# First feed-forward: ScalarE copies the first expert's rows, and the gate's last operation goes behind the masked outputs

## The chip, the cores and the metric

The kernel runs on one core of a Trainium2 chip. The metric is the device time of one launch in microseconds (us). Three runs of the kernel before gave 2103.96, 2107.25 and 2112.59 us, median 2107.25 us. Five engines work side by side, each through its own list of instructions in order: TensorE (PE, with its weight loads PEld), VectorE (DVE), ScalarE (ACT), GpSimd (POOL) and SyncE (SP, which issues transfers here). They meet only at semaphores: a producer counts one up, a consumer waits until it has reached a value.

## What is computed

A stack of four layers, each with an attention and a gated feed-forward, over 64 sequences of 64 tokens with 128 features. Each layer adds `tanh(gate) * block(layernorm(x))` to `x`. The change touches only the first feed-forward, an attention whose values and outputs go through one of 8 experts for each token and head:

```python
q = (x @ w_q).reshape(b, n, HEADS, DIM_HEAD).transpose(0, 2, 1, 3)      # 8 heads of 64
k = (x @ w_k).reshape(b, n, HEADS, DIM_HEAD).transpose(0, 2, 1, 3)
gates = jax.nn.sigmoid((x @ w_gate).reshape(b, n, HEADS, EXPERTS).transpose(0, 2, 1, 3))
sel = jnp.argmax(gates, axis=-1)
gm = jax.nn.one_hot(sel, EXPERTS, dtype=x.dtype) * gates
values = jnp.einsum('bhne,ehdk,bnd->bhnk', gm, value_experts, x)
sim = jnp.einsum('bhid,bhjd->bhij', q * SCALE, k)
sim = jnp.where(causal_mask, jnp.finfo(sim.dtype).min, sim)
attn = jax.nn.softmax(sim, axis=-1)
out = jnp.einsum('bhij,bhjk->bhik', attn, values)
out = jnp.einsum('bhne,ehkd,bhnk->bhnd', gm, output_experts, out)
return out.sum(axis=1)
```

## The kernel before

The 4096 tokens are 32 tiles of 128 (two sequences each), and 4 tiles make a group: 8 groups, of which groups 1 to 6 run as one loop. `l0_ffn` writes the list of each engine by hand, and these lists set the order. Count for tile t of group g:

- **Values.** TensorE multiplies the tile by the value weights of each of the 8 experts (`expert_values`, L1011, two passes of one multiplication each), into three PSUM banks in turn. VectorE takes them out in `pick`: a plain copy of expert 0 into `val` (L1228), then seven predicated copies (L1233), each of which overwrites the heads that chose this expert. Each pick waits for the one before it, since all write the same rows; TensorE may write expert e only when the bank's last content is taken.
- **Scores.** `scores` (L1021, L1027), then on VectorE `softmax`: row maximum (L1242) and difference (L1245); on ScalarE `exp` (L1141); on VectorE `totals` (L1251 to L1256, sum, reciprocal, times the gate) and `scale_probs` (L1262), placed behind the first and the second predicated copy of the next tile. TensorE turns the probabilities (L1037), ScalarE copies them (`copy_pT`, L1148), TensorE multiplies by the gated values (`values`, L1053), ScalarE copies the result (`copy_oT`, L1154). GpSimd multiplies the picked values by the gate (L955).
- **Once a group.** In tile 0, ScalarE also copies the turned one-hots (`copy_onehots`, L1161), from which SyncE makes the masks by transfers; in tile 1, VectorE applies a norm (L247) and ScalarE copies its turned rows (L271).
- **End of a group.** TensorE computes the next group's logits and projects its q and k (L1002), which ScalarE copies. VectorE's `pick_experts` makes the one-hots from the logits and ends with the gate's last operation (L1218): gate = 0.5 * tanh + 0.5. That one waits for the tanh (L1134), which ScalarE computes behind its last k copy. Only then come the 32 masked outputs (`masked_outputs`, L1271, z = oT * mask, in three buffers), each of which TensorE multiplies by an output expert's weights into one accumulator (`output_experts`, L1062). ScalarE copies the accumulator (L1183), and the next group's tile 0 follows on TensorE and VectorE.

Of the kernel before, what the change touches and what calls it, by code (L numbers as in the profile page):

```python
# [78 lines left out]
def count(n):  # L79

    return n + 1
# [767 lines left out]
def l0_ffn(core, nc, d):  # L849
# [17 lines left out]
    with ExitStack() as ctx:  # L867
# [36 lines left out]
                                                                sem("oh_turned"), sem("ohT_ready"))  # L904
        qk_done, qk_copied = sem("qk_done"), sem("qk_copied")
        ve_done, pick_done, v2_ready = sem("ve_done"), sem("pick_done"), sem("v2_ready")
        score_done, sub_done, exp_done, tot_done = sem("score_done"), sem("sub_done"), sem("exp_done"), sem("tot_done")
        p_turned, pT_ready, pv_done, prob_ready = sem("p_turned"), sem("pT_ready"), sem("pv_done"), sem("prob_ready")
        oT_ready, z_done = sem("oT_ready"), sem("z_done")
# [6 lines left out]
        with nc.Block() as block:  # L916
# [19 lines left out]
            @block.gpsimd  # L936
            def _(pool):
                nc.gpsimd.tensor_copy(causal[:, :], core.const("caus_n")).then_inc(setup_done, 1)
                nc.gpsimd.memset(oh_bf[:, :, :], 0.0).then_inc(setup_done, 1)

                def stage(u):
                    after(pool, ve_done, u * G * E)
                    nc.gpsimd.tensor_copy(xs[:, :], core.xnT[:, bass.ds(u * GT, GT)]).then_inc(xs_ready, 1)

                gate = top[:, 2, :].rearrange("p (t h) -> p t h", t=G)

                def gate_values(g, t):
                    n = g * G + t
                    pool.wait_ge(pick_done, count((n + 1) * E))
                    after(pool, pv_done, n - 1)  # L950
                    for b in range(2):
                        for a in range(2):
                            r = slice(b * SEQ, (b + 1) * SEQ)
                            after(pool, v2_ready, n * 4 + 2 * b + a)
                            nc.gpsimd.tensor_tensor(  # L955
                                v2[a * SEQ:(a + 1) * SEQ, t % 2, b, :, :],
                                val[r, t % 2, :, :].rearrange("p (c a) k -> p c a k", a=2)[:, :, a, :],
                                bcast(gate[r, t, :].rearrange("p (c a) -> p c a", a=2)[:, :, a], 2, HD),
                                ALU.mult).then_inc(v2_ready, 1)
                    pool.wait_ge(v2_ready, count(n * 4 + 4))  # L960

                def group(g, more):
                    for t in range(1, G):
                        if t == G - 1 and more:
                            stage(g + 1)
                        gate_values(g, t)
                    if more:
                        gate_values(g + 1, 0)
                        norm_gpsimd(core, nc, pool, ns, g)

                stage(0)
                norm_gpsimd(core, nc, pool, edge, 0)
                gate_values(0, 0)
                group(0, True)
                pool.wait_ge(edge.ready, count(1))
                with pool.Fori(1, GROUPS - 1) as g:
                    group(g, True)
                group(GROUPS - 1, False)

            @block.tensor  # L980
            def _(pe):
# [12 lines left out]
                def project(u, chunks):  # L994

                    for i in chunks:
                        c = i % C
                        if i < 2:
                            after(pe, pick_done, u * G * E)
                        else:  # L1000
                            pe.wait_ge(qk_copied, count(u * 2 * C + i - 1))
                        nc.tensor.matmul(work[i % 2][:, :], (wq, wk)[i // C][:, c * P:(c + 1) * P],  # L1002
# [2 lines left out]
                def expert_values(g, t, between=None, later=None):  # L1005
                    for e in range(E):
                        n = (g * G + t) * E + e
                        if e == 2 and t == 0:
                            pe.wait_ge(y_ready, count(g))
                        after(pe, pick_done, n - 1 if e < 2 else n - 2)  # L1010
                        nc.tensor.matmul(value_banks[e % 3][:, :], xs[:, t * P:(t + 1) * P], ve[:, e, :],  # L1011
                                         start=True, stop=True).then_inc(ve_done, 1)
                        if e == 2 and between:
# [42 lines left out]

                def output_experts(g):
                    pe.wait_ge(y_ready, count(g))
                    pe.wait_ge(pick_done, count((g + 1) * G * E))
                    for n in range(C * E):  # L1060
                        pe.wait_ge(z_done, count(g * C * E + n + 1))
                        nc.tensor.matmul(acc[:, :], oe[:, n % E, n // E, :], z[:, n % Z, :], start=(n == 0),  # L1062
# [54 lines left out]
            def _(act):  # L1117
# [8 lines left out]
                def copy_k(u, chunks):  # L1126
                    after(act, score_done, u * G)
                    for c in chunks:
                        act.wait_ge(qk_done, count(u * 2 * C + C + c + 1))
                        nc.scalar.activation(kT[:, c, :], work[c % 2][:, :], ACT.Copy).then_inc(qk_copied, 1)  # L1130

                def gate_tanh(u):
                    act.wait_ge(top_ready, count(u + 1))
                    nc.scalar.activation(top[:, 1, :], top[:, 0, :], ACT.Tanh, scale=0.5).then_inc(tanh_done, 1)  # L1134
# [27 lines left out]

                def group(g, more, normed=True):
                    for t in range(G - 1):
                        copy_pT(g, t)
                        exp(g, t + 1)
                        copy_oT(g, t)
# [14 lines left out]
                    act.wait_ge(y_turned, count(g))  # L1182
                    nc.scalar.activation(yT[:, :], acc[:, :], ACT.Copy).then_inc(y_ready, 1)  # L1183
                    if more:
                        exp(g + 1, 0)

                copy_q(0, range(C))
                copy_k(0, range(C))
                gate_tanh(0)
                edge_scalar(core, nc, act, edge, misc)  # L1190
                exp(0, 0)
                group(0, True, False)
                with act.Fori(1, GROUPS - 1) as g:
                    group(g, True)
# [3 lines left out]
            def _(dve):  # L1198
# [4 lines left out]
                def pick_experts(u):  # L1203
# [9 lines left out]
                    after(dve, oh_turned, u)  # L1213
                    nc.vector.tensor_copy(oh_bf[:, :, 0:H * E], oh[:, :, :].rearrange("p (t h) e -> p t (h e)", t=G))\
                        .then_inc(oh_ready, 1)
                    dve.wait_ge(tanh_done, count(u + 1))

                    ch.link(nc.vector.tensor_scalar(top[:, 2, :], top[:, 1, :], 0.5, 0.5, ALU.mult, ALU.add))  # L1218
                    ch.done()

                def pick(g, t, between=()):
                    for e in range(E):
                        n = (g * G + t) * E + e
                        dve.wait_ge(ve_done, count(n + 1))
                        w3 = value_banks[e % 3][:, :].rearrange("p (h k) -> p h k", h=H)
                        if e == 0:
                            after(dve, v2_ready, (g * G + t - 1) * 4)
                            nc.vector.tensor_copy(val[:, t % 2, :, :], w3).then_inc(pick_done, 1)  # L1228
                        else:
                            dve.wait_ge(pick_done, count(n))  # L1230
                            dve.sem_inc(may_pick, 1)
                            m_e = bcast(oh[:, t * H:(t + 1) * H, e], 2, HD).bitcast(I32)
                            nc.vector.copy_predicated(val[:, t % 2, :, :], m_e, w3).then_inc(pick_done, 1)  # L1233
                        if 0 < e <= len(between):
                            between[e - 1]()

                def softmax(g, t):
# [47 lines left out]
                def group(g, more, normed=True):  # L1285
# [5 lines left out]
                    totals(g, G - 1)  # L1291
                    scale_probs(g, G - 1)
                    if more:
                        pick_experts(g + 1)
                    masked_outputs(g)
                    if more:
                        pick(g + 1, 0)
                    add_to_x(g, more)
                    if more:
                        softmax(g + 1, 0)  # L1300

                edge_measure(core, nc, dve, edge)
                pick_experts(0)
                edge_apply(core, nc, dve, edge)
                pick(0, 0)
                softmax(0, 0)
# [2106 lines left out]
```

## Time and profile before

| what | value |
|---|---|
| three runs, median | 2107.25 us |
| the profiled execution, its own time | 2104.33 us |
| its span, first to last instruction | 2102.2 us |
| mean granted TensorE clock | 0.950 |
| busy share of the span: PE, DVE, ACT, POOL | 91%, 73%, 40%, 34% |

The span is the profiled execution without its start and end (2.1 us). "Busy" is time in which an engine had an instruction in it. "Granted clock" is the TensorE clock that the chip gave: 1.00 is 2.4 GHz, 0.5 is 1.2 GHz. A row of the timeline has the start in us, the duration, the engine, the line, the operation with output and inputs, how many were merged, and in brackets how long the engine had been idle before it and who ended that.

### The profile page before, as it was taken

The numbers are of one execution on the slowest core, as the hardware profiler recorded it, in microseconds if no ns is written. First come the engines' busy times: TensorE is split into PE (matmuls) and PEld (weight loads), VectorE is DVE, ScalarE is ACT, GpSimd is POOL, SyncE is SP. The second block draws the span as 40 slices with busy tenths as digits, with TensorE's granted clock in tenths as the row PEclk, the third lists the DMA queues.
The fourth block names the chain that finished last, engine by engine and source line by source line (L and its number), as shares of the span: only waits on it lengthen the run. The fifth ranks groups of instructions, "written<-read, shape, count | busy, mean of one in ns | idle before, by whom it ended". The sixth has DMA issues, their size and how long they took to land. (4 is left out here: it accounts for less than half of the span.)

```text
span 2102.2 us, 41789 instructions
## 1 busy us (share of the span) xinstructions
PE 1916.6 (91%) x14339; PEld 1025.3 (49%) x14339; DVE 1537.1 (73%) x3177; ACT 836.1 (40%) x1500; POOL 721.2 (34%) x953
## 2 busy tenths in 40 slices
PE   5869999998998988999999999979998999989975
PEld 3734444444444444555555554435663444436641
DVE  4767877877877776777777776857785666768978
ACT  6622112112012005666666663315652223225655
POOL 2541111102112105677676774455730000013222
PEclk9569999999999999999999999989998999999985
DMA  5403203212132041000000000000002524221001
GB/s 140 149 1 82 63 21 79 45 39 61 35 66 61 20 113 76 2 2 1 0 0 0 0 2 1 1 8 15 15 7 80 129 73 118 63 64 20 16 1 40
DMA packets 60080, 89.74 MB, mean 43 GB/s; under 512 B 23720, under 2 KB 42024, under 8 KB 55472
## 3 DMA queue, kind: packets, MB, share of 16 engines
q1 hardware_dynamic: 59952, 88.10, 17.1%
q8 instruction: 72, 1.18, 0.2%
q14 instruction: 56, 0.46, 0.1%
HBM read 80.91 MB, written 2.97 MB: 40 GB/s over the span
## 5 line engine op out<-in xcount | busy, mean ns | idle before, releaser
L955 POOL TENSOR_TENSOR l0f_v<-l0f_val,l0f_top 64x256 f32<-64x256 f32 x128 | 78.2, 611 | 484.2 <-DVE l0f_val L1233 476.7
L1062 PE MATMUL l0f_acc<-l0f_z,w_all 128*128 128x512 f32 x512 | 228.5, 608 | 15.0 <-DVE l0f_z L1271 15.0
L1011 PE MATMUL l0f_work<-w_all,l0f_xs 128*128 128x512 f32 x384 | 183.4, 600 | 15.0 <-DVE l0f_val L1228 14.2
L1062 PEld LDWEIGHTS l0f_acc<-l0f_z,w_all 128*128 128x128 f32 x512 | 99.0, 195 | 143.9 <-issue 123.1
L255 POOL TENSOR_SCALAR var_eps<-mean_var 128x4 f32<-128x4 f32 (+1 forms) x64 | 16.8, 263 | 375.8 <-DVE mean_var L239 373.6
L1477 PE MATMUL l1x_proj_v<-l1x_wvo,l1x_cs 128*64 128x512 f32 x512 | 139.2, 622 | 0.0
L1233 DVE COPY_PREDICATED l0f_val<-l0f_oh,l0f_work 128x512 f32<-128x512 int32 x160 | 116.7, 729 | 22.8 <-PE l0f_work L1011 7.9
L2881 ACT ACTIVATE l2f_act_g<-l2f_pg 128x512 f32<-128x512 f32 x104 | 61.6, 594 | 146.3 <-PE l2f_pu L2816 134.3
L2824 PE MATMUL l2f_acc<-l2f_hid,w_all 128*128 128x512 f32 x208 | 107.4, 598 | 10.2 <-DVE l2f_hid L2962 10.2
L2956 DVE TENSOR_TENSOR l2f_hu<-l2f_act_g,l2f_pu 128x512 f32<-128x512 f32 x104 | 71.1, 684 | 60.3 <-ACT l2f_act_g L2881 58.8
L1011 PEld LDWEIGHTS l0f_work<-w_all,l0f_xs 128*128 128x128 f32 x384 | 66.1, 190 | 87.8 <-issue 32.2
L2815 PE MATMUL l2f_pg<-xnT_all,w_all 128*128 128x512 f32 x208 | 108.7, 605 | 0.0
L2535 ACT ACTIVATE a_probT<-a_pT 128x512 f32<-128x512 f32 x128 | 76.3, 596 | 81.1 <-PE a_pT L2412 81.1
L1271 DVE TENSOR_TENSOR l0f_z<-l0f_oT,l0f_first_mask 128x512 f32<-128x512 f32 x128 | 87.2, 691 | 28.4 <-PE l0f_acc L1062 22.6
L2816 PE MATMUL l2f_pu<-xnT_all,w_all 128*128 128x512 f32 x208 | 107.9, 601 | 0.0
L1402 POOL TENSOR_TENSOR l1x_rs_q<-l1x_ms_q,minus_half 128x8 f32<-128x8 f32 x64 | 104.7, 1636 | 5.7 <-POOL l1x_ms_q L1398 0.8
L1411 POOL TENSOR_TENSOR l1x_rs_k<-l1x_ms_k,minus_half 128x8 f32<-128x8 f32 x64 | 104.7, 1636 | 5.3
L1271 DVE TENSOR_TENSOR l0f_z<-l0f_oT,w_all 128x512 f32<-128x512 f32 x128 | 88.6, 692 | 21.2 <-PE l0f_acc L1062 20.9
L1631 ACT ACTIVATE l1x_vo<-l1x_proj_v 128x512 f32<-128x512 f32 x128 | 76.4, 597 | 62.5 <-PE l1x_proj_v L1477 62.5
L1712 DVE TENSOR_TENSOR l1x_nm_q<-l1x_proj_q,l1x_rs_q 128x512 f32<-128x512 f32 x64 | 44.3, 692 | 77.8 <-POOL l1x_rs_q L1402 77.8
L1415 POOL TENSOR_TENSOR l1x_prob<-l1x_prob,l1x_inv 128x512 f32<-128x512 f32 x64 | 66.7, 1042 | 98.2 <-DVE l1x_inv L1741 98.2
L1183 ACT ACTIVATE xn<-l0f_acc 128x512 f32<-128x512 f32 x8 | 4.8, 597 | 237.9 <-PE l0f_acc L1062 237.9
(400 smaller groups left out, 4375.2 us busy)
## 6 DMA issues: line engine op xcount, KB each, us to landing
l0f_first_mask<-onehots SPq DMA_DIRECT2D x32, 512.0 KB, 5.8
w_all<-onehots SPq DMA_DIRECT2D x32, 512.0 KB, 11.8
w_all<-combination SPq DMA_DIRECT2D x40, 256.0 KB, 5.1
w_all<-in_weights SPq DMA_DIRECT2D x1, 4640.0 KB, 16.8
l0x_m_b<-running_max SPq DMA_DIRECT2D x16, 256.0 KB, 4.3
w_all<-combination SPq DMA_DIRECT2D x16, 224.0 KB, 4.3
w_all<-combination SPq DMA_DIRECT2D x16, 192.0 KB, 4.1
w_all<-combination SPq DMA_DIRECT2D x16, 160.0 KB, 4.1
```

The lines of the kernel that those rows point to most:

```text
L955: nc.gpsimd.tensor_tensor(v2[a * SEQ:(a + 1) * SEQ, t % 2, b, :, :], val[r, t % 2, :, :].rearrange("p (c a) k -> p c a k", a=2)[:, :, a, : ...
L1011: nc.tensor.matmul(value_banks[e % 3][:, :], xs[:, t * P:(t + 1) * P], ve[:, e, :], start=True, stop=True).then_inc(ve_done, 1)
L1062: nc.tensor.matmul(acc[:, :], oe[:, n % E, n // E, :], z[:, n % Z, :], start=(n == 0), stop=(n == C * E - 1)).then_inc(acc_done, 1)
L1233: nc.vector.copy_predicated(val[:, t % 2, :, :], m_e, w3).then_inc(pick_done, 1)
L1271: nc.vector.tensor_tensor(z[:, n % Z, :], oT[:, n // E, :], masks[n // E][:, n % E, :], ALU.mult)\
L1402: nc.gpsimd.tensor_tensor(rs_q[:, :], ms_q[:, 1, :], core.half[:, 0:HU], ALU.pow).then_inc(rs_q_done, 1)
L1411: nc.gpsimd.tensor_tensor(rs_k[:, :], ms_k[:, 1, :], core.half[:, 0:HU], ALU.pow).then_inc(rs_k_done, 1)
L1477: ins = nc.tensor.matmul(proj_v[a * SEQ:(a + 1) * SEQ, :], cs[:, j // 4, at:at + SEQ], wvo[:, h, a, :], start=True, stop=True)
L1631: nc.scalar.activation(vo[:, j % 2, b, :, :], proj_v[:, :].rearrange("p (c d) -> p c d", c=C), ACT.Copy)\
L2815: nc.tensor.matmul(pg[n % 3][:, :], wg[:, c * P:(c + 1) * P], x_of(g), start=True, stop=True)
L2816: nc.tensor.matmul(pu[n % 3][:, :], wu[:, c * P:(c + 1) * P], x_of(g), start=True, stop=True)\
L2824: nc.tensor.matmul(acc[:, :], wd[:, c * P:(c + 1) * P], hid[:, n % 3, :], start=(c == 0), stop=(c == CH - 1)).then_inc(acc_done, 1)
```

## The change

Three things are moved.

1. The copy of expert 0 into `val` leaves VectorE's `pick` and becomes `copy_first` on ScalarE, with a semaphore of its own, `first_copied`. The picks now count 7 a tile. TensorE's fourth expert of a tile waits for `first_copied`, and so does VectorE's first predicated copy.
2. `copy_first` of the next tile stands at the head of what ScalarE does for a tile: ahead of `copy_pT` and of the next tile's exponential. In tile 0 the group's first exponential, which stood at the end of the group before, comes behind the copy for tile 1. The copy for tile 0 of the next group is behind the accumulator's copy.
3. The gate's last operation is cut out of `pick_experts` (`gate_halves`) and stands behind the 32 masked outputs, ahead of the next group's picks.

```diff
                 def expert_values(g, t, between=None, later=None):
                     for e in range(E):
                         n = (g * G + t) * E + e
+                        if e == 0 and t == 0:
+                            pe.wait_ge(qk_copied, count((g + 1) * 2 * C))
                         if e == 2 and t == 0:
                             pe.wait_ge(y_ready, count(g))
-                        after(pe, pick_done, n - 1 if e < 2 else n - 2)
+                        if e == 3:
+                            pe.wait_ge(first_copied, count(g * G + t + 1))
+                        else:
+                            after(pe, pick_done, (g * G + t) * PICKS + (-1, 0, -2, 0, 1, 2, 3, 4)[e])
...
+                def copy_first(g, t):
+                    n = g * G + t
+                    act.wait_ge(ve_done, count(n * E + 1))
+                    after(act, v2_ready, (n - 1) * 4)
+                    nc.scalar.activation(val[:, t % 2, :, :], value_banks[0][:, :].rearrange("p (h k) -> p h k", h=H),
+                                         ACT.Copy).then_inc(first_copied, 1)
...
                 def group(g, more, normed=True):
                     for t in range(G - 1):
+                        copy_first(g, t + 1)
+                        if t == 0:
+                            exp(g, 0)
                         copy_pT(g, t)
                         exp(g, t + 1)
                         copy_oT(g, t)
...
                     if more:
-                        exp(g + 1, 0)
+                        copy_first(g + 1, 0)
...
+                def gate_halves(u, ch):
                     dve.wait_ge(tanh_done, count(u + 1))
-
                     ch.link(nc.vector.tensor_scalar(top[:, 2, :], top[:, 1, :], 0.5, 0.5, ALU.mult, ALU.add))
                     ch.done()
...
                     if more:
-                        pick_experts(g + 1)
+                        ch = pick_experts(g + 1)
                     masked_outputs(g)
                     if more:
+                        gate_halves(g + 1, ch)
                         pick(g + 1, 0)
                     add_to_x(g, more)
```

How the lists of the engines change is shown at three places. First VectorE at the end of group 0, from the one-hots' cast to the next group's picks. Before (lines L1218 gate, L1271 masked outputs, L1228 first expert's copy):

```order
L1214 CAST l0f_oh_bf<-l0f_oh 128x4x64 [waits counter1_24,counter1_20]
L1218 TENSOR_SCALAR l0f_top<-l0f_top 128x32 [waits counter1_22]
L1271 TENSOR_TENSOR l0f_z<-l0f_oT,l0f_first_mask 128x512 [waits mask_loaded0,counter1_42,counter1_39,counter1_20]
L1271 TENSOR_TENSOR l0f_z<-l0f_oT,l0f_first_mask 128x512 [waits counter1_42] x7
...
L1271 TENSOR_TENSOR l0f_z<-l0f_oT,l0f_first_mask 128x512 [waits counter1_42] x7
L1228 COPY l0f_val<-l0f_work 128x512 [waits counter1_30,counter1_28]
L1233 COPY_PREDICATED l0f_val<-l0f_oh,l0f_work 128x512 [waits counter1_28,counter1_29]
```

And now, at the same place (L1237 gate, L1289 masked outputs, L1251 predicated copy; counter1_40 is `oT_ready`, counter1_22 `tanh_done`, counter1_31 `first_copied`):

```order
L1231 CAST l0f_oh_bf<-l0f_oh 128x4x64 [waits counter1_24,counter1_20]
L1289 TENSOR_TENSOR l0f_z<-l0f_oT,l0f_first_mask 128x512 [waits counter1_43,mask_loaded0,counter1_40]
L1289 TENSOR_TENSOR l0f_z<-l0f_oT,l0f_first_mask 128x512 [waits counter1_43] x7
...
L1289 TENSOR_TENSOR l0f_z<-l0f_oT,l0f_first_mask 128x512 [waits counter1_43] x7
L1237 TENSOR_SCALAR l0f_top<-l0f_top 128x32 [waits counter1_22]
L1251 COPY_PREDICATED l0f_val<-l0f_oh,l0f_work 128x512 [waits counter1_31,counter1_20,counter1_28]
```

The gate's operation and its wait for ScalarE moved from ahead of 32 instructions to behind them, and the copy of expert 0 is gone from the list.

Second, VectorE at a tile's turn, from the difference of one tile to the totals, before:

```order
L1245 TENSOR_TENSOR l0f_diff<-l0f_score,l0f_mx 128x2x4x64 [waits counter1_48]
L1228 COPY l0f_val<-l0f_work 128x512 [waits counter1_28]
L1233 COPY_PREDICATED l0f_val<-l0f_oh,l0f_work 128x512 [waits counter1_28,counter1_29]
L1251 TENSOR_REDUCE l0f_tot<-l0f_prob 128x8 [waits counter1_33]
L1253 RECIPROCAL l0f_tot<-l0f_tot 128x8 [waits counter1_49]
```

and now (counter1_34 is `exp_done`):

```order
L1263 TENSOR_TENSOR l0f_diff<-l0f_score,l0f_mx 128x2x4x64 [waits counter1_34,counter1_49]
L1251 COPY_PREDICATED l0f_val<-l0f_oh,l0f_work 128x512 [waits counter1_28,counter1_31]
L1269 TENSOR_REDUCE l0f_tot<-l0f_prob 128x8 [waits counter1_34]
L1271 RECIPROCAL l0f_tot<-l0f_tot 128x8 [waits counter1_50]
```

One instruction instead of two stands between the difference and the sum of its exponentials, and the first predicated copy waits for ScalarE.

Third, ScalarE in the loop body, tiles 0 and 1, before (L1148 turned probabilities, L1141 exponential, L1154 output, L1161 one-hots, L271 norm):

```order
L1148 ACTIVATE l0f_probT<-l0f_turn 128x512 [waits counter1_37]
...
L1141 ACTIVATE l0f_prob<-l0f_diff 128x512 [waits counter1_34,counter1_35,counter1_32]
...
L1154 ACTIVATE l0f_oT<-l0f_po 128x4x128 [waits counter1_40]
...
L1161 ACTIVATE l0f_ohT<-l0f_misc 128x512 [waits onehots_stored]
L1148 ACTIVATE l0f_probT<-l0f_turn 128x512 [waits counter1_37,counter1_35]
...
L1154 ACTIVATE l0f_oT<-l0f_po 128x4x128 [waits counter1_40,counter1_37]
...
L271 ACTIVATE xnT_all<-l0f_misc 128x512
```

and now (L1143 `copy_first`, L1162 turned probabilities, L1155 exponential, L1168 output, L1175 one-hots):

```order
L1143 ACTIVATE l0f_val<-l0f_work 128x512 [waits counter1_30]
...
L1155 ACTIVATE l0f_prob<-l0f_diff 128x512 [waits counter1_35,counter1_36,counter1_33]
L1162 ACTIVATE l0f_probT<-l0f_turn 128x512 [waits counter1_38,counter1_36]
...
L1155 ACTIVATE l0f_prob<-l0f_diff 128x512 [waits counter1_35,counter1_36,counter1_33]
...
L1168 ACTIVATE l0f_oT<-l0f_po 128x4x128 [waits counter1_41]
...
L1175 ACTIVATE l0f_ohT<-l0f_misc 128x512 [waits onehots_stored]
...
L1143 ACTIVATE l0f_val<-l0f_work 128x512 [waits counter1_30]
L1162 ACTIVATE l0f_probT<-l0f_turn 128x512 [waits counter1_38,counter1_36]
...
L271 ACTIVATE xnT_all<-l0f_misc 128x512
...
L1143 ACTIVATE l0f_val<-l0f_work 128x512 [waits counter1_30]
```

The copy for tile 1 comes ahead of tile 0's exponential; the copy for tile 2 is behind the exponential of tile 1, the output copy and the one-hots; the copy for tile 3 is behind the exponential of tile 2, the output copy and the norm's rows.

## Rows read from the trace of the kernel before

**Rows 1.** Stretches of one group each: us, busy time by engine, clock, DMA share, GB/s.
```profile
221.30:302.20 80.90, 75.46 (x445) 36.43 (x444) 63.14 (x110) 13.29 (x24) 11.65 (x19) 1.00 0.25 54
302.20:385.30 83.10, 77.29 (x445) 37.00 (x445) 63.38 (x110) 13.35 (x25) 11.65 (x19) 0.98 0.24 52
...
630.10:712.90 82.80, 77.26 (x446) 37.02 (x445) 63.23 (x110) 13.34 (x25) 11.65 (x19) 0.98 0.24 51
```

**Rows 2.** Who waited for whom, stretch 140 to 780: us, times, longest.
```profile
PE l0f_acc L1062 <- DVE l0f_z L1271: 15.0, 8, 1.9
```

**Rows 3.** Timeline where group 3's masked outputs begin: start, duration, engine, line.
```profile
515.69 1.98 PE L1002 MATMUL l0f_work<-xnT_all,w_all 128*128 x4
519.61 4.11 PE L1062 MATMUL l0f_acc<-l0f_z,w_all 128*128 128x512 f32 x5 [1.94 <-DVE l0f_z L1271]
...
515.81 0.60 ACT L1154 ACTIVATE l0f_oT<-l0f_po 128x512 f32<-128x512 f32 x1 [0.49 <-PE l0f_po L1053]
...
518.46 0.18 DVE L1218 TENSOR_SCALAR l0f_top<-l0f_top 128x32 f32<-128x32 f32 x1 [3.84 <-ACT l0f_top L1134]
518.87 1.89 DVE L1271 TENSOR_TENSOR l0f_z<-l0f_oT,l0f_first_mask 128x512 f32<-128x512 f32 x3 [0.22 <-DVE l0f_top L1218]
```

**Rows 4.** Timeline, last group, where no gate operation stands ahead.
```profile
760.84 0.60 ACT L1154 ACTIVATE l0f_oT<-l0f_po 128x512 f32<-128x512 f32 x1 [2.15 <-PE l0f_po L1053]
...
761.47 1.89 DVE L1271 TENSOR_TENSOR l0f_z<-l0f_oT,l0f_first_mask 128x512 f32<-128x512 f32 x3 [4.12 <-ACT l0f_oT L1154]
```

**Rows 5.** Line L1062 in two groups: us, PE busy, clock, DMA share, GB/s.
```profile
438.50:466.20 27.70, 27.66 (x64) 1.00 0.18 38
519.60:549.00 29.40, 29.39 (x64) 0.94 0.16 36
```

**Rows 6.** Timeline, VectorE and TensorE, tiles 0 and 1 of that group.
```profile
467.29 0.69 DVE L1228 COPY l0f_val<-l0f_work 128x512 f32<-128x512 f32 x1 [2.86 <-PE l0f_work L1011]
...
477.41 0.69 DVE L1245 TENSOR_TENSOR l0f_diff<-l0f_score,l0f_mx 128x512 f32<-128x512 f32 x1
478.02 0.69 DVE L1228 COPY l0f_val<-l0f_work 128x512 f32<-128x512 f32 x1
478.85 0.73 DVE L1233 COPY_PREDICATED l0f_val<-l0f_oh,l0f_work 128x512 f32<-128x512 int32 x1
479.47 0.67 DVE L1251 TENSOR_REDUCE l0f_tot<-l0f_prob 128x8 f32<-128x512 f32 x1
...
478.77 1.98 PE L1011 MATMUL l0f_work<-w_all,l0f_xs 128*128 128x512 f32 x4 [1.53 <-DVE l0f_val L1228]
```

**Rows 7.** Timeline, VectorE, tile 3, whose totals have no pick ahead.
```profile
508.02 0.69 DVE L1245 TENSOR_TENSOR l0f_diff<-l0f_score,l0f_mx 128x512 f32<-128x512 f32 x1
509.41 0.69 DVE L1251 TENSOR_REDUCE l0f_tot<-l0f_prob 128x8 f32<-128x512 f32 x1 [0.69 <-ACT l0f_prob L1141]
```

**Rows 8.** Timeline, ScalarE and VectorE, tiles 2 and 3 of that group.
```profile
487.90 0.58 ACT L1154 ACTIVATE l0f_oT<-l0f_po 128x512 f32<-128x512 f32 x1
488.38 0.59 ACT L1161 ACTIVATE l0f_ohT<-l0f_misc 128x512 bf16<-128x512 bf16 x1
...
490.05 0.73 DVE L1233 COPY_PREDICATED l0f_val<-l0f_oh,l0f_work 128x512 f32<-128x512 int32 x1
...
499.60 0.59 ACT L271 ACTIVATE xnT_all<-l0f_misc 128x512 f32 x1
...
500.21 0.73 DVE L1233 COPY_PREDICATED l0f_val<-l0f_oh,l0f_work 128x512 f32<-128x512 int32 x1 [0.22 <-PE l0f_work L1011]
```

**Rows 9.** Timeline, ScalarE and VectorE, tiles 2 and 3 of group 0.
```profile
164.27 0.59 ACT L1161 ACTIVATE l0f_ohT<-l0f_misc 128x512 bf16<-128x512 bf16 x1
...
164.66 0.73 DVE L1233 COPY_PREDICATED l0f_val<-l0f_oh,l0f_work 128x512 f32<-128x512 int32 x1 [0.31 <-PE l0f_work L1011]
...
173.62 0.58 ACT L1154 ACTIVATE l0f_oT<-l0f_po 128x512 f32<-128x512 f32 x1
...
174.30 0.73 DVE L1233 COPY_PREDICATED l0f_val<-l0f_oh,l0f_work 128x512 f32<-128x512 int32 x1 [0.31 <-PE l0f_work L1011]
```

More of the change, by code:

```diff
@@ L906, in l0_ffn @@
         ve_done, pick_done, v2_ready = sem("ve_done"), sem("pick_done"), sem("v2_ready")
+        first_copied = sem("first_copied")
+        PICKS = E - 1
         score_done, sub_done, exp_done, tot_done = sem("score_done"), sem("sub_done"), sem("exp_done"), sem("tot_done")
@@ L948, in gate_values @@
                     n = g * G + t
-                    pool.wait_ge(pick_done, count((n + 1) * E))
+                    pool.wait_ge(pick_done, count((n + 1) * PICKS))
                     after(pool, pv_done, n - 1)
@@ L998, in project @@
                         if i < 2:
-                            after(pe, pick_done, u * G * E)
+                            after(pe, pick_done, u * G * PICKS)
                         else:
@@ L1058, in output_experts @@
                     pe.wait_ge(y_ready, count(g))
-                    pe.wait_ge(pick_done, count((g + 1) * G * E))
+                    pe.wait_ge(pick_done, count((g + 1) * G * PICKS))
                     for n in range(C * E):
@@ L1189, in _ @@
                 gate_tanh(0)
+                copy_first(0, 0)
                 edge_scalar(core, nc, act, edge, misc)
-                exp(0, 0)
                 group(0, True, False)
@@ L1215, in pick_experts @@
                         .then_inc(oh_ready, 1)
+                    return ch
+                def gate_halves(u, ch):
                     dve.wait_ge(tanh_done, count(u + 1))
@@ L1221, in pick @@
                 def pick(g, t, between=()):
-                    for e in range(E):
-                        n = (g * G + t) * E + e
-                        dve.wait_ge(ve_done, count(n + 1))
+                    n = g * G + t
+                    for e in range(1, E):
+                        dve.wait_ge(ve_done, count(n * E + e + 1))
                         w3 = value_banks[e % 3][:, :].rearrange("p (h k) -> p h k", h=H)
-                        if e == 0:
-                            after(dve, v2_ready, (g * G + t - 1) * 4)
-                            nc.vector.tensor_copy(val[:, t % 2, :, :], w3).then_inc(pick_done, 1)
-                        else:
[L1230 to L1234, printed above, removed]
+                        if e == 1:
+                            dve.wait_ge(first_copied, count(n + 1))
+                        else:
+                            dve.wait_ge(pick_done, count(n * PICKS + e - 1))
+                        dve.sem_inc(may_pick, 1)
+                        m_e = bcast(oh[:, t * H:(t + 1) * H, e], 2, HD).bitcast(I32)
+                        nc.vector.copy_predicated(val[:, t % 2, :, :], m_e, w3).then_inc(pick_done, 1)
+                        if e <= len(between):
                             between[e - 1]()
@@ L1302, in _ @@
                 edge_measure(core, nc, dve, edge)
-                pick_experts(0)
+                gate_halves(0, pick_experts(0))
                 edge_apply(core, nc, dve, edge)
```

## The prediction

> **What bounds the kernel now.** I read the chip's clock by stretches first: it splits the first feed-forward into its 8 groups. A steady group takes 80.9 us with TensorE busy for 75.5, VectorE for 63.1 and ScalarE for only 13.3 [rows 1]. So TensorE is the bound, ScalarE has room, and a microsecond is won only where TensorE waits. The stretches also show two kinds of group: 80.9 us at clock 1.00, and 82.8 to 83.1 us at 0.98 [rows 1].
>
> The list of waits was next: TensorE waits for the first masked output 8 times, 15.0 us in all, at most 1.94 [rows 2]. Seven times 1.94 are 13.6; the rest is the last group's, which has no next group behind it. The timeline shows why [rows 3]. The output copy ends at 515.81 + 0.60 = 516.41, and VectorE has everything that a masked output needs. It sits idle for 3.84 us all the same, because the gate's operation at 518.46 stands ahead and waits for ScalarE's tanh, which is queued behind the last k copies. The first masked output begins at 518.87. TensorE is through with its projections at 517.67 and stands for 1.94.
>
> In three groups (those of 302, 466 and 630) this wait costs twice: behind it TensorE gets the lower of its clocks for a while. The 64 passes of L1062 take 29.4 us at a mean clock of 0.94 in the group of 466, and 27.7 at 1.00 in the one before [rows 5]: 1.7 us.
>
> In tiles 1 to 3 VectorE sets the pace, with TensorE waiting for it for up to 1.53 us [rows 6]. There the copy of expert 0 costs VectorE 478.85 - 478.02 = 0.83 us per tile, since the first predicated copy waits for it to end [rows 6].
>
> **The change part by part.**
>
> *Gate behind the masked outputs.* What the masked outputs wait for last is then the output copy. The last group, which has no gate operation there, shows the lag: copy ends at 760.84 + 0.60 = 761.44, first masked output at 761.47 [rows 4]; the masks had landed there too. So in a steady group the first one starts at 516.45 instead of 518.87 and ends at 517.14, ahead of TensorE's 517.67. The wait of 1.94 is gone, in 7 groups: **-13.6**. The gate's 0.18 us now stand behind the last masked output, where VectorE was idle for 2.86 us before the copy at 467.29 [rows 6], and the tanh is long done: 0. GpSimd needs the gate only behind the picks. If the cover were gone it would cost 7 x 0.2 = 1.4.
>
> *The clock.* The group of 466 lacks about 0.06 x 29.4 = 1.8 us of clock in L1062's stretch [rows 5], and a group at 0.98 lacks 0.02 x 83 = 1.7 in all [rows 1]: the low stretch stands behind the wait and nowhere else. With the wait gone I take them as gone: 3 x 1.7, **-5.1**. Bounds: 0, if something else brings the clock down, to -5.1.
>
> *Copy for tile 0 on ScalarE.* VectorE waited for TensorE there anyway (2.86 us [rows 6]), and both go on at one expert per 0.86 us: 0. ScalarE copies behind the accumulator's copy, well before expert 1 is there.
>
> *Copy for tile 1, ahead of the exponential.* TensorE's expert 0 is ready while VectorE still adds to x, so the first predicated copy starts where the plain copy did, 478.02. The totals, then, can't begin before the exponential is done. Where no pick stands between, difference to totals takes 509.41 - 508.02 = 1.39 [rows 7]; before it was 479.47 - 477.41 = 2.06 here [rows 6]. Gain 0.67, not 0.83.
>
> *Copy for tile 2.* It stands behind the exponential, the output copy and the one-hots. ScalarE starts such operations one per 0.5 us (487.90 to 488.38 [rows 8]). The copy starts at 488.38 + 0.50 - 0.67 = 488.21, ends 0.60 later at 488.81, and with 0.15 for the semaphore the first predicated copy starts at 488.96 instead of 490.05: 1.09 ahead.
>
> *Copy for tile 3.* It stands behind the exponential, the output copy and the norm's copy: 499.60 + 0.50 - 1.09 + 0.60 + 0.15 = 499.76 instead of 500.21. Only 0.45 is left of the lead, because VectorE waits for ScalarE here where it waited for TensorE before. TensorE's fourth and later experts follow the picks with the same lead. So 0.45 a group, groups 1 to 7 (the last is built alike): **-3.1**.
>
> *Group 0* has no norm on VectorE behind which the copies could hide. Tile 2: 164.27 + 0.50 + 0.60 + 0.15 = 165.52 against 164.66, 0.86 late. Tile 3: 173.62 + 0.86 + 0.50 + 0.60 + 0.15 = 175.73 against 174.30, 1.43 late [rows 9]. **+1.4**.
>
> The step from one ScalarE operation to the next is the unsure figure. Taken at its full 0.60 plus 0.10, each of the three steps from the exponential to the copy is 0.2 longer and the end 0.1: 0.7 later in all. Tile 2 is then 1.09 - 0.7 = 0.4 ahead, tile 3 499.60 + 0.50 - 0.4 + 0.60 + 0.15 + 0.7 = 501.15, 0.94 late, 6.6 in 7 groups; group 0 has 0.7 more in tile 2 and some 0.5 in tile 3, 2.7. That makes the tiles +9.3 instead of -1.7. On the other side, if the copies never come late, tiles 1 to 3 gain about 0.67 + 0.83 and what TensorE leaves of the third, 1.5 a group in 7 groups and 0 in group 0: -10.5. I take the middle, since the rows of two neighbouring operations show the 0.5 directly.
>
> ScalarE's copy of 128x512 from PSUM takes 0.60 (the output copy at 515.81 [rows 3]) against 0.69 on VectorE [rows 6]. The Trainium skill advises the opposite ("ScalarE: Activation LUTs", rules for kernel authors): plain element-wise work belongs on VectorE, which it calls up to about three times as fast in bf16. This operand is fp32, and the rows show ScalarE the quicker one here. At three times 0.69, 2.07 us, the copies of tiles 2 and 3 would each be 1.47 later in 8 groups, +23.5, and the whole +3 instead of a gain; the trace disagrees with that.
>
> **Sum:** -13.6 - 5.1 - 3.1 + 1.4 = -20.4. The profiled execution took 2104.33 us (span 2102.2 and 2.1 around it), so 2083.9; it lies 2.9 below the median of the three runs, 2107.25. From the median, 2107.25 - 20.4 = **2087**.
>
> **The rivals.**
>
> *The tiles gain in full* (ScalarE never late): -13.6 - 5.1 - 10.5 = -29.2, 2078. For: ScalarE is idle most of the time. Against: its three operations ahead of the copy all start at the same moment, when the difference is done.
>
> *The low clock stays or comes elsewhere*: -15.3, 2092. For: it came in only three of the seven groups with the same wait, so something besides the wait decides.
>
> *ScalarE's queue at its long step*: -18.7 + 9.3 = -9.4, 2098. For: each operation waits for its own semaphores. Against: the 0.48 between neighbours [rows 8].
>
> *The change doesn't open the wait*: masked outputs wait for something else at 516 (a mask, the accumulator), and only the tiles' -1.7 is left, 2105.5. Against: rows 4.
>
> *Slower*: the waits move into the tiles and pull the clock down there. TensorE's fourth expert no longer waits, but the fifth waits some 0.8 us for the first pick, the sixth 0.9 for the second, in 21 tiles (three in each of 7 groups), and longer with the long step. Each low stretch costs 1.7. Starting from the -9.4 of the long step, 6 such stretches eat the gain, and 12 make it slower by over 0.5%. Two in each of 7 groups: -9.4 + 23.8 = +14.4, 2121.7. For: three stretches behind a wait of 1.94. Against: the wait of 1.53 in tile 1 [rows 6] left the clock at 1.00 in the groups of 80.9.
>
> **How the numbers follow.** Forecast as worked out, 2083 to 2092: 0.50. Tiles in full, 0.12. Low clock stays, 0.15. Long step, 0.13. Nothing opened, 0.04. Slower, 0.06. What a measurement of this kernel can tell from no change is about 0.5%, 10.5 us, so faster means below 2096.7: 0.50 + 0.12 + 0.15 and a fourth of the long step's, 0.80. Same: the rest of the long step and the unopened wait, 0.14. Slower by over 10.5: 0.06. The range 2079 to 2099 takes in the forecast, the low clock, most of the long step and about half of the full gain, and leaves out under 2 in 10.
>
> **What will show it.** Right: no wait of L1062's first pass for VectorE in groups 0 to 6; the first masked output within 0.1 us of the output copy's end; clock 1.00 in the groups of 302, 466 and 630; all steady groups at 78.5 us (80.9 - 1.94 - 0.45); difference to totals 1.4 us in tile 1; the first predicated copies of tiles 2 and 3 waiting for `copy_first`; group 0 longer in its tiles by about 1.4. Wrong: TensorE still waiting at 516 to 518 for a masked output; a clock below 1.00 inside the tiles; steps of 0.7 or more between the exponential, the output copy and `copy_first`; or a later stage that gives back what this one wins, though each begins only when the one before it is through.

## The result and the profile after

| | before | changed |
|---|---|---|
| median | 2111.98 us (7 runs) | 2097.23 us (7 runs) |
| lowest to highest | 2103.96 to 2118.68 | 2092.68 to 2100.41 |
| span of the profiled execution | 2102.2 | 2093.9 |

The ratio is 0.9934, 95% interval 0.9919 to 0.9949, so 0.7% faster: the medians differ by 14.8 us, and the interval is 10.8 to 17.1 us. Forecast were 20.4 us less, 2087 us, range 2079 to 2099.

The wait that the change was about is gone. TensorE, VectorE and ScalarE in the timeline of the changed kernel where group 4's masked outputs begin [answers to rows 3, which are group 4's too; their heading counts it as group 3]; a row has start, duration, engine, line, operation, and in brackets the idle time before it and who ended it:

```profile
509.77 1.98 PE L1004 MATMUL l0f_work<-xnT_all,w_all 128*128 x4
511.59 27.63 PE L1069 MATMUL l0f_acc<-l0f_z,w_all 128*128 128x512 f32 x64
...
508.48 0.29 DVE L1231 CAST l0f_oh_bf<-l0f_oh 128x256 bf16<-128x256 f32 x1
510.70 2.64 DVE L1289 TENSOR_TENSOR l0f_z<-l0f_oT,l0f_first_mask 128x512 f32<-128x512 f32 x4 [1.93 <-ACT l0f_oT L1168]
...
536.68 0.69 DVE L1289 TENSOR_TENSOR l0f_z<-l0f_oT,l0f_first_mask 128x512 f32<-128x512 f32 x1 [0.17 <-PE l0f_acc L1069]
537.29 0.17 DVE L1237 TENSOR_SCALAR l0f_top<-l0f_top 128x32 f32<-128x32 f32 x1
541.18 0.73 DVE L1251 COPY_PREDICATED l0f_val<-l0f_oh,l0f_work 128x512 f32<-128x512 int32 x1 [3.71 <-PE l0f_work L1018]
...
509.88 0.60 ACT L1168 ACTIVATE l0f_oT<-l0f_po 128x512 f32<-128x512 f32 x1 [0.49 <-PE l0f_po L1060]
```

VectorE begins at 510.70, 0.22 behind the output copy's end (510.48; the prediction had asked for 0.1), and TensorE goes from its projections to the 64 passes with no wait. Between 140 and 780 us it now waits once for a masked output, 1.5 us in the last group, where it had waited 8 times and 15.0 us. The gate's 0.17 us stand in an idle stretch of 3.7 us.

By stretches, three groups of the changed kernel (us, then busy time of PE, PEld, DVE, ACT, POOL, the clock, DMA share, GB/s) [answers to rows 1]:

```profile
222.71:301.24 78.53, 75.42 (x445) 36.32 (x444) 60.51 (x106) 15.44 (x29) 11.68 (x19) 1.00 0.25 56
459.10:539.26 80.16, 76.87 (x445) 37.14 (x444) 60.48 (x106) 15.44 (x29) 11.67 (x19) 0.98 0.25 53
539.26:618.11 78.85, 75.45 (x445) 36.33 (x444) 60.51 (x106) 15.46 (x28) 11.68 (x19) 1.00 0.25 54
```

A steady group takes 78.8 us instead of 80.9 to 81.1 (forecast 78.5), and one group has a low stretch instead of three. But look at VectorE and ScalarE: VectorE has 2.6 us less to do and ScalarE 2.1 more, and of that nothing shows in the 78.8: the wait alone accounts for what a steady group gained.

The same group of 459 by its two parts, from the accumulator's copy to the first output product and from there to the next copy (us, PE busy, clock, DMA share, GB/s), and then the first part of the group behind it [answers to rows 5]:

```profile
459.10:511.60 52.50, 49.21 (x381) 0.97 0.29 61
511.60:539.30 27.70, 27.70 (x66) 1.00 0.17 38
539.30:590.40 51.10, 47.70 (x380) 1.00 0.30 63
```

The low stretch has moved: not behind the masked outputs' start any more, but inside the first part, in the tiles, where it costs 1.4 us (52.5 against 51.1). VectorE and ScalarE in tiles 1 to 3 of the group of 539 [answers to rows 6 and 8]:

```profile
550.52 0.69 DVE L1263 TENSOR_TENSOR l0f_diff<-l0f_score,l0f_mx 128x512 f32<-128x512 f32 x1
551.24 0.72 DVE L1251 COPY_PREDICATED l0f_val<-l0f_oh,l0f_work 128x512 f32<-128x512 int32 x1
551.91 0.69 DVE L1269 TENSOR_REDUCE l0f_tot<-l0f_prob 128x8 f32<-128x512 f32 x1
...
562.19 0.72 DVE L1251 COPY_PREDICATED l0f_val<-l0f_oh,l0f_work 128x512 f32<-128x512 int32 x1 [0.29 <-ACT l0f_val L1143]
...
570.12 0.69 DVE L1263 TENSOR_TENSOR l0f_diff<-l0f_score,l0f_mx 128x512 f32<-128x512 f32 x1
573.08 0.73 DVE L1251 COPY_PREDICATED l0f_val<-l0f_oh,l0f_work 128x512 f32<-128x512 int32 x1 [2.27 <-ACT l0f_val L1143]
...
570.84 0.63 ACT L1155 ACTIVATE l0f_prob<-l0f_diff 128x512 f32<-128x512 f32 x1 [3.79 <-DVE l0f_diff L1263]
571.38 0.58 ACT L1168 ACTIVATE l0f_oT<-l0f_po 128x512 f32<-128x512 f32 x1
571.86 0.59 ACT L271 ACTIVATE xnT_all<-l0f_misc 128x512 f32 x1
572.34 0.60 ACT L1143 ACTIVATE l0f_val<-l0f_work 128x512 f32<-128x512 f32 x1
```

Difference to totals is 1.39 us in tile 1, as forecast. In tile 3 VectorE waits 2.27 us for the copy, which has three of ScalarE's operations ahead of it, each 0.48 to 0.54 behind the one before. Where VectorE had waited for TensorE in the kernel before, it now waits for ScalarE.

TensorE's second wait in tile 1 of the kernel before (the first, 1.53 us, is in rows 6), and both waits of the changed kernel:

```profile
481.43 1.12 PE L1011 MATMUL l0f_acc<-w_all,l0f_xs 128*128 128x512 f32 x2 [0.68 <-DVE l0f_val L1233]
```

```profile
552.02 1.12 PE L1018 MATMUL l0f_work<-w_all,l0f_xs 128*128 128x512 f32 x2 [0.99 <-DVE l0f_val L1251]
...
553.96 1.12 PE L1018 MATMUL l0f_acc<-w_all,l0f_xs 128*128 128x512 f32 x2 [0.82 <-DVE l0f_val L1251]
```

### The profile page after: what moved, and what is told of

It reads as the page before. It is cut to its first block and busy times, and to the rows that moved or that the text cites. A ratio compares the mean times of both kernels' runs of the same rounds, so it can differ in the third digit from the quotient of the medians.

```text
span 2093.9 us, 41926 instructions
## 1 busy us (share of the span) xinstructions
PE 1922.9 (92%) x14337; PEld 1031.1 (49%) x14339; DVE 1514.5 (72%) x3145; ACT 853.1 (41%) x1532; POOL 722.6 (35%) x953
## 5 line engine op out<-in xcount | busy, mean ns | idle before, releaser
L1069 PE MATMUL l0f_acc<-l0f_z,w_all 128*128 128x512 f32 x512 | 223.1, 597 | 1.5 <-DVE l0f_z L1289 1.5
L1251 DVE COPY_PREDICATED l0f_val<-l0f_oh,l0f_work 128x512 f32<-128x512 int32 x160 | 116.6, 729 | 69.3 <-PE l0f_work L1018 33.3
L255 POOL TENSOR_SCALAR var_eps<-mean_var 128x4 f32<-128x4 f32 (+1 forms) x64 | 16.9, 264 | 381.7 <-DVE mean_var L239 379.5
L1289 DVE TENSOR_TENSOR l0f_z<-l0f_oT,l0f_first_mask 128x512 f32<-128x512 f32 x128 | 87.1, 691 | 36.7 <-PE l0f_acc L1069 18.1
L1289 DVE TENSOR_TENSOR l0f_z<-l0f_oT,w_all 128x512 f32<-128x512 f32 x128 | 88.6, 692 | 21.3 <-PE l0f_acc L1069 20.9
L2643 DVE TENSOR_REDUCE a_mx<-a_score 128x16 f32<-128x1024 f32 x64 | 77.6, 1212 | 23.8 <-PE a_score L2417 22.0
```

The lines of the kernel that those rows point to most:

```text
L1289: nc.vector.tensor_tensor(z[:, n % Z, :], oT[:, n // E, :], masks[n // E][:, n % E, :], ALU.mult)\
L2643: nc.vector.tensor_reduce(mx[:, t % 2, :], score[t % 2][:, :].rearrange("p (h k) -> p h k", h=H), AX.X, ALU.max).then_inc(max_done, 1)
```

## Experiments

Five theories were open: (a) the gain is the gate's alone; (b) the copies bring their part; (c) the low stretches hang on the wait; (d) the copies lose by their place in ScalarE's list; (e) the rest is lost in later stages. "First part" is from the accumulator's copy to the first output product, "second part" from there to the next copy.

**The gate's operation alone.** On the kernel before:

```diff
+                        if e == 0 and t == 0:
+                            pe.wait_ge(qk_copied, count((g + 1) * 2 * C))
...
-                        pick_experts(g + 1)
+                        ch = pick_experts(g + 1)
                     masked_outputs(g)
                     if more:
+                        gate_halves(g + 1, ch)
                         pick(g + 1, 0)
```

> The kernel before with only the gate's last operation behind the masked outputs (and the wait of the first expert's multiplication for ScalarE's last k copies, which that order needs); the copies of expert 0 stay on VectorE. My theory: TensorE's wait of 1.94 us at the first masked output goes in 7 groups and the low stretches of the clock behind it go too, so the steady groups' first part (accumulator copy to first output product) falls from 53.3 to 51.3 us, the first feed-forward from 647.5 us (first tanh to last accumulator copy) to about 629, and the time by 18.6 us, ratio 0.991. Rival, the later stages give back part of whatever this stage wins, by whatever reason: same stage time, but a ratio of 0.994 to 0.996 and the stretch behind the stage longer than 1310.6 us by 5 or more.

Measured: 2090.92 us against 2109.26, ratio 0.9912, interval 0.9894 to 0.9929. First and second part of a steady group at full clock, and ahead of them group 0's first part from its tanh on:

```profile
145.40:192.80 47.40, 46.82 (x376) 1.00 0.31 69
457.30:508.40 51.10, 47.57 (x380) 1.00 0.29 63
508.40:536.10 27.70, 27.70 (x66) 1.00 0.16 38
```

No group has a low stretch but the last. The first feed-forward took 628.0 us instead of 647.5, and the ratio is the 0.991 that was expected, not the 0.994 to 0.996 of the rival; the stretch behind this stage took 1315.5 us, though, which the last experiment takes up. So by the trace this edit alone brings 2.4 us more than the whole change (630.4; the intervals of the two ratios overlap). Of the 2.4, the changed kernel loses 1.7 in group 0 and 1.4 by its low stretch in a tile, and wins 0.6 in group 1. The steady first part, 51.1, is the same as the changed kernel's: in groups 3 to 6 the moved copies bring nothing.

**The copies alone.** The changed kernel with

```diff
-                        ch = pick_experts(g + 1)
+                        gate_halves(g + 1, pick_experts(g + 1))
                     masked_outputs(g)
                     if more:
-                        gate_halves(g + 1, ch)
                         pick(g + 1, 0)
```

> The changed kernel with the gate's last operation back ahead of the masked outputs, so that only the copies of expert 0 are moved. My theory: the wait of 1.94 us at the first masked output is back in 7 groups, the tiles of a steady group are shorter by only 0.2 us (53.3 to 53.1 in the first part), group 0's first part is 1.6 longer than before (49.3 to 50.9), and low stretches of the clock stay at about three; the time is the same as before within 0.2%. Rival, the copies are where the gain of the change comes from: 0.996 or less. Rival, the copies cost the missing part: 1.002 or more.

Measured: 2114.08 against 2109.26, ratio 1.0020, interval 1.0008 to 1.0032: slower, at the edge between my "same within 0.2%" and the rival's cost, and the rival is nearer. Group 0's first part is 51.1 us. Of the steady groups, one row of a first and one of a second part:

```profile
389.40:442.60 53.20, 47.97 (x381) 1.00 0.28 60
...
606.20:635.70 29.50, 29.50 (x65) 0.94 0.16 36
```

The first part is 53.2, as good as unchanged (53.3 before). The stage took 653.8 us instead of 647.5. The cost is group 0's 1.8 and more low stretches: five second parts have one instead of three, and one first part too, besides the last group's. I had expected about three. Why there are more is not shown.

**TensorE kept busy through the wait.** On the kernel before:

```diff
                         project(g + 1, range(C + 2, 2 * C))
+                        for _ in range(2):
+                            nc.tensor.matmul(turn[:, :], wq[:, 0:P], core.xnT[:, 0:GT], start=True, stop=True)
```

> The kernel before, with two extra multiplications of 128x512 (0.43 us a pass, two passes each) into a free bank behind the last k projection, whose result nobody reads: TensorE is busy for 1.7 of the 1.94 us that it waited for the first masked output. The masked outputs still begin behind the gate's operation. My theory: the first output product starts where it did (53.3 us behind the accumulator's copy), but the clock doesn't fall, so the second part of all groups is 27.7 us instead of 29.4 in three of them: 5 us less, ratio 0.9976. Rival, the low stretches have nothing to do with the wait: three groups with 29.4 us stay, ratio 1.000.

Measured: 2105.18 against 2109.26, ratio 0.9985, interval 0.9974 to 0.9995. TensorE and VectorE in the timeline, and the two parts of that group:

```profile
516.57 1.88 PE L1097 MATMUL l0f_turn<-xnT_all,w_all 128*128 128x512 f32 x4
518.67 2.84 PE L1062 MATMUL l0f_acc<-l0f_z,w_all 128*128 128x512 f32 x6 [0.22 <-DVE l0f_z L1273]
...
517.52 0.18 DVE L1220 TENSOR_SCALAR l0f_top<-l0f_top 128x32 f32<-128x32 f32 x1 [3.81 <-ACT l0f_top L1136]
```

```profile
465.40:518.70 53.30, 49.48 (x385) 1.00 0.28 60
518.70:546.40 27.70, 27.70 (x65) 1.00 0.18 38
```

The first product starts where it did, since VectorE still waits for the tanh, yet no second part but the last group's is 29.4 or longer: all are at clock 1.00. That is theory (c), shown by itself, in the seven groups of one profiled execution, and the interval of the ratio lies below 1. The stage is 643.3 us instead of 647.5, 4.2 less of 5 expected; the last group, whose low stretch is longer, takes back 1.0.

**The copies right behind the exponential.** On the changed kernel:

```diff
                     for t in range(G - 1):
-                        copy_first(g, t + 1)
                         if t == 0:
+                            copy_first(g, 1)
                             exp(g, 0)
                         copy_pT(g, t)
                         exp(g, t + 1)
+                        if t + 2 < G:
+                            copy_first(g, t + 2)
                         copy_oT(g, t)
```

> The changed kernel with the copies of expert 0 for tiles 2 and 3 moved ahead of the output copy: right behind the exponential of the tile before, so two of ScalarE's operations no longer stand before them. My theory: VectorE's wait for the copy goes from 0.3 us to 0 in tile 2 and from 2.3 to about 1.4 in tile 3, a steady group's first part falls from 51.2 to about 50.0 us, group 0's from 49.1 to about 47.5, and the time is some 10 us below the changed kernel, ratio to the kernel before 0.989. Rival, the output copy and what hangs on it (the turned probabilities, the next group's projections) are late then and take it back: first part 51.2 or more.

Measured: 2086.03 against 2109.26, ratio 0.9895, interval 0.9877 to 0.9914. Tile 3 on VectorE and ScalarE, and a steady group's two parts:

```profile
562.58 0.69 DVE L1265 TENSOR_TENSOR l0f_diff<-l0f_score,l0f_mx 128x512 f32<-128x512 f32 x1
564.93 0.73 DVE L1253 COPY_PREDICATED l0f_val<-l0f_oh,l0f_work 128x512 f32<-128x512 int32 x1 [1.66 <-PE l0f_work L1018]
...
563.31 0.63 ACT L1155 ACTIVATE l0f_prob<-l0f_diff 128x512 f32<-128x512 f32 x1 [3.80 <-DVE l0f_diff L1265]
563.95 0.60 ACT L1143 ACTIVATE l0f_val<-l0f_work 128x512 f32<-128x512 f32 x1
564.45 0.59 ACT L1168 ACTIVATE l0f_oT<-l0f_po 128x512 f32<-128x512 f32 x1
```

```profile
454.30:504.40 50.10, 47.23 (x380) 1.00 0.30 64
504.40:532.10 27.70, 27.70 (x66) 1.00 0.17 38
```

The copy is done at 564.55, and what VectorE waits for in tile 3 is TensorE again. The first part is 50.1 to 50.2 (50.0 expected) and group 0's 47.8 (from 49.1). Theory (d) holds, and the output copy that was pushed back costs little: at most the 0.1 to 0.2 us by which the first part missed what was expected.

**Picks counted by 8 again.** On that kernel; the thresholds of TensorE and GpSimd follow:

```diff
-                    n = g * G + t
                     for e in range(1, E):
-                        dve.wait_ge(ve_done, count(n * E + e + 1))
+                        n = (g * G + t) * E + e
+                        dve.wait_ge(ve_done, count(n + 1))
...
-                            dve.wait_ge(pick_done, count(n * PICKS + e - 1))
+                            dve.wait_ge(pick_done, count(n))
...
-                        nc.vector.copy_predicated(val[:, t % 2, :, :], m_e, w3).then_inc(pick_done, 1)
+                        nc.vector.copy_predicated(val[:, t % 2, :, :], m_e, w3).then_inc(pick_done, 2 if e == 1 else 1)
```

> The kernel with the copies right behind the exponential, and the picks counted by 8 a tile again (the first predicated copy counts two up), so that VectorE's two waits ahead of a predicated copy follow from one register, as before the change, and not from two. My theory: the extra register instruction ahead of each predicated copy in the loop body is what made its step 0.875 us instead of 0.86 and the first one behind the totals 0.1 later; the steps go back, tile 0's first part and tiles 1 to 3 are 0.1 each shorter, a steady group's first part falls from 50.2 to about 49.8 us, 2 to 3 us in all, ratio 0.988. Rival, the steps come from ScalarE and VectorE meeting at the same memory: steps stay at 0.875 and the first part at 50.2.

Measured: 2084.74 against 2109.45, ratio 0.9884, interval 0.9863 to 0.9904; the interval overlaps that of the kernel without it, so by the time alone the two aren't told apart. The trace tells them apart. The picks of tile 1 behind the totals in the kernel without it (the first fence) and in this one (the second), and this one's first part:

```profile
545.70 0.17 DVE L1276 TENSOR_TENSOR l0f_tot<-l0f_tot,l0f_top 128x8 f32<-128x8 f32 x1
546.01 0.72 DVE L1253 COPY_PREDICATED l0f_val<-l0f_oh,l0f_acc 128x512 f32<-128x512 int32 x1
...
547.22 1.60 DVE L1253 COPY_PREDICATED l0f_val<-l0f_oh,l0f_work 128x512 f32<-128x512 int32 x2
548.97 0.73 DVE L1253 COPY_PREDICATED l0f_val<-l0f_oh,l0f_acc 128x512 f32<-128x512 int32 x1
```

```profile
544.10 0.17 DVE L1275 TENSOR_TENSOR l0f_tot<-l0f_tot,l0f_top 128x8 f32<-128x8 f32 x1
544.34 0.72 DVE L1252 COPY_PREDICATED l0f_val<-l0f_oh,l0f_acc 128x512 f32<-128x512 int32 x1
...
545.55 1.59 DVE L1252 COPY_PREDICATED l0f_val<-l0f_oh,l0f_work 128x512 f32<-128x512 int32 x2
547.27 0.73 DVE L1252 COPY_PREDICATED l0f_val<-l0f_oh,l0f_acc 128x512 f32<-128x512 int32 x1
...
453.30:503.00 49.70, 47.33 (x380) 1.00 0.30 65
```

Two picks in a row take 548.97 - 547.22 = 1.75 us there and 1.72 here, and the one behind the totals comes 0.31 and 0.24 later. In all the first part of a steady group falls by 0.4 to 0.5 us, from 50.1 or 50.2 to 49.7. The edit changes only how the counts come about: in the loop the changed kernel has two register instructions ahead of each predicated copy, the kernel before and this one have one. This kernel's median is the lowest of the study.

What in it takes the time is another matter. The traces also hold the register and semaphore instructions, which the profile's views leave out. Between two picks of the kernel before, one semaphore instruction waits for both counts and is already waiting when the pick ends (a step of 0.862 us, median of 79). In the changed kernel the two waits stand on two instructions, and the one with the last wait begins 0.04 us behind the pick's end (0.875, median of 78); the register instructions were through 0.40 us before that end. Where both register instructions stand ahead of the pick before, the waits are apart all the same, and the step is 0.870 (median of 18). So between picks it is mostly the split of the waits that shows; only behind the totals does the second register instruction, 0.05 us long, stand in the way itself. No run separates the two.

**The same kernels again.** Nothing edited; the stretch behind the first feed-forward is the question.

> The kernel before, unchanged. If the low stretches of the clock behind the first feed-forward follow from the program alone, the stretch from its last accumulator copy to the end is 1310.6 us again within 1 us. If they are the chance of a run, it differs by several us, and the 6.9 us by which this stretch was longer in the profile of the changed kernel say nothing of the change.

> The kernel before, a third time, for the spread of the stretch behind the first feed-forward: within 1 us of the other two if it follows from the program, several us off if not. The number of groups with a low stretch behind the wait of 1.94 us: three of seven if the group's period sets it, anything from two to five if the chip's own phase does.

> The changed kernel, unchanged. By the program alone: 1317.5 us behind the first feed-forward again, and the low stretch in a tile of group 4 (at 474 us) again. By chance: the one moves by several us and the other comes in another group or not at all, while the stretches at full clock (51.15 us first part, 27.67 second) repeat to 0.05.

Times 2109.8, 2109.69 and 2090.45 us. From the last accumulator copy to the end, one row for each execution (us, then as above): the kernel before, first, again, third; then the changed kernel, first and again:

```profile
791.70:2102.20 1310.50, 1219.25 (x9575) 658.97 (x9575) 951.54 (x2008) 657.26 (x1110) 566.86 (x734) 0.96 0.11 29
```

```profile
793.70:2107.90 1314.20, 1222.04 (x9573) 662.64 (x9575) 951.77 (x2008) 656.97 (x1110) 566.92 (x734) 0.96 0.12 29
```

```profile
793.40:2107.80 1314.40, 1221.07 (x9573) 660.53 (x9575) 951.54 (x2008) 656.78 (x1110) 566.89 (x734) 0.96 0.12 29
```

```profile
776.40:2093.90 1317.50, 1225.80 (x9574) 663.55 (x9575) 950.82 (x2008) 657.23 (x1110) 568.07 (x734) 0.95 0.12 29
```

```profile
774.40:2088.60 1314.20, 1222.46 (x9573) 661.29 (x9575) 950.82 (x2008) 656.84 (x1110) 566.90 (x734) 0.96 0.11 29
```

The same program differs by 4 us there, and two of the three of before equal one of after within 0.2. The 7.0 us by which the two first profiles differ can't be put down to the change. Before's three executions have three low second parts each besides the last group's: twice in groups 2, 4 and 6, once in 1, 4 and 6. The changed kernel's low stretch in a tile came in group 3 the second time, and again just once.

## Why the prediction was right, and where it was off

The direction and the main cause were right, and the time fell into the range. The size was forecast at 20.4 and measured at 14.8 (10.8 to 17.1). The kernel before, forecast from 2107.25, came out at 2111.98 over seven runs, which together with the smaller gain puts 2097.23 near the range's upper end. Within the first feed-forward the traces leave less in doubt than the medians: from its first tanh to its last accumulator copy it took 647.5 us before (three executions, within 0.2) and 630.4 in the changed kernel (two, within 0.2), 17.1 less. Against the steps of the sum:

- *The wait, -13.6.* Right, and somewhat more. In groups 3 to 6 the first part fell by 53.28 - 51.15 = 2.13 us where only the gate moved, and the second by 0.1; over all 7 groups it was -15.2. What was missed: idle time is counted from a pass's end, while without a wait the next pass starts before that end (64 passes in 27.63 us are 0.43 each, though four in a row take 1.88, so one lasts 0.59); and four passes behind a wait take 1.98 instead of 1.88.
- *The clock, -5.1.* Right for the three stretches, by both the gate's edit and the filled wait.
- *The tiles, -3.1.* This is the term that failed: it measured 0 in groups 3 to 6 (51.15 us with the copies moved and with them left), -0.6 in group 1 and +0.2 in group 2, -0.4 in all. The steps for tile 1 (1.39 us from difference to totals) and for ScalarE's queue (0.48 to 0.54 a step, 0.15 to the pick) were right. Counted from the group's start, the first predicated copies of tiles 1, 2 and 3 were to come 0.83, 1.09 and 0.45 us earlier; they came 0.56, 0.81 and 0.08 earlier (at 551.24, 562.19 and 573.08 in the group of 539.26, against 478.85, 490.05 and 500.21 in the group of 466.31). Mis-sized was the pace of the picks, which the sum took as unchanged: with the counts from two registers it is 0.875 us, and 0.07 more behind the totals. Putting it back brought 0.4 to 0.5 us a group, about the lead that was to be left; this was measured with the copies behind the exponential, not on the changed kernel itself. The sum counted only what computes.
- *Group 0, +1.4.* Measured +1.7 (47.4 to 49.1).
- *Left out of the sum:* a low stretch in one tile, +1.4, and the last group, 0.7 longer in the first profile: there the clock stands at 0.50 to 0.51 from 740.5 to 750.8, 10.3 us, where before it was 758.7 to 765.6, 6.9 us. Why is open; it is as long with the gate's edit alone. The stretch in the tile fits the slower rival's mechanism, at one place instead of the 12 that it needed, and was listed as a sign of being wrong; that the waits there bring it is not shown, since no run fills them. TensorE's waits in tile 1 were 1.53 and 0.68 before and are 0.99 and 0.82 now. Apart from the last group, the low stretch came into the tiles once in each of four executions that have the copies on ScalarE (changed kernel twice, copies alone, copies behind the exponential), once not (picks by 8), and in none of the five without (kernel before three times, gate alone, filled wait).

-15.2 - 5.1 - 0.4 + 1.7 + 1.4 + 0.7 = -16.9, against 17.1 less measured. That the total came out no further from the forecast is in part luck: the wait brought 1.6 us more than was summed, while the tiles brought 2.7 less. The 2.3 us between the stage's 17.1 and the medians' 14.8 are not explained; 17.1 is the upper end of the interval. Whether the later stages return some of it is open: the executions there spread over 4 us for the same kernel, and the kernels with the shortest first stage had 1315 to 1318 us behind it, the kernel before 1311 to 1314, but the one with the filled wait 1321.

The wait sum stands on the right reading of one row: an idle VectorE with nothing missing but its turn. The copies' sum stood on rows as well, and was off by what no row of busy time shows.

## What to carry to other kernels

An operation that waits for another engine and isn't needed yet belongs behind the work that could go on; here one operation of 0.18 us held 32 others and cost 2.1 us a group, plus the clock behind it. Work given to an idle engine is only as good as its place in that engine's list: put it ahead of what is released at the same moment, or the receiver trades one wait for another. In a chain of short dependent operations inside a loop, look also at how the counts of the waits come about, and let those of neighbouring waits come from one register: here that was worth 0.4 to 0.5 us a group.

## What the hardware showed that was not expected

TensorE waited 1.94 us and was then granted its lower clock (1.2 GHz) for a while in three of seven equal groups, and in the other four not; with the wait filled by two multiplications that nobody needed it stayed at the higher (2.4 GHz) in all seven, and the kernel was 0.15% faster for doing more work. Counts from two registers instead of one showed as 0.013 us in the step from pick to pick, though VectorE computes for 0.73 us of each 0.86. The register instructions were indeed through 0.40 us before the pick ended; what came later was the instruction with the second of the two waits.
